# A fused attention and feed-forward kernel: normalised rows reach their columns through HBM, and the order of the projections changes

## The reference, cut to what matters

```python
query = layernorm(x) @ w_q.T + b_q          # 16 heads of 32
key_, value = ctx @ w_k.T + b_k, ctx @ w_v.T + b_v
attn = softmax(causal(query @ key_.T / sqrt(32)))
x = x + tanh(g_xattn) * ((attn @ value) @ w_o.T + b_o)
z = mx_quantize(layernorm(x))               # blocks of 32, grid of a 6 bit float
x = x + tanh(g_ffn) * (z @ mx_quantize(w_f).T + b_f)
```

## Time and profile before

| | |
|---|---|
| median of 3 runs | 1390.96 us |
| profiled execution | 1392.38 us |
| its span in the trace | 1390.6 us |
| TensorE busy | 1354.2 us, 97% |
| VectorE, GpSimd, ScalarE busy | 1124.7, 938.7, 916.6 us |
| mean granted TensorE clock | 0.989 of 2.4 GHz |

### The profile page before, as it was taken

One profiled execution on the slowest core, in us unless ns is written; L12 is line 12 of the kernel. 1 busy time (PEld: TensorE's weight loads), 2 busy tenths in 40 slices (PEclk: granted clock), 3 DMA queues, 4 the chain that ended last, 5 costly groups with the idle time before them and its releaser, 6 DMA issues.

```text
span 1390.6 us, 34895 instructions
## 1 busy us (share of the span) xinstructions
PE 1354.2 (97%) x10608; PEld 1198.5 (86%) x10608; DVE 1124.7 (81%) x4219; ACT 916.6 (66%) x2969; POOL 938.7 (68%) x1449
## 2 busy tenths in 40 slices
PE   7899999999999999999999999999999999999987
PEld 7788888898888888888888888888888889889865
DVE  5768888788888888888878878888888888888773
ACT  4667666667666666667666667666666666766661
POOL 1657776677676777676677676677677667767564
PEclk9999999999999999999999999999999999999998
DMA  8444344444444444434444434444444444443320
GB/s 253 118 112 107 103 111 124 118 129 107 109 109 120 124 128 117 107 101 119 121 126 123 108 99 115 126 119 124 110 106 109 126 118 128 110 116 99 88 62 31
DMA packets 181912, 159.10 MB, mean 114 GB/s; under 512 B 30176, under 2 KB 164320, under 8 KB 181728
## 3 DMA queue, kind: packets, MB, share of 16 engines
q1 hardware_dynamic: 181728, 156.88, 43.3%
HBM read 39.33 MB, written 16.78 MB: 40 GB/s over the span
## 4 chain that ended last, share of the span: by engine, by line
PE 59%; DVE 20%; SPq 9%; issue 5%; DMA 3%; ACT 1%; POOL 1%; DVEq 0%; ACTq 0%; POOLq 0%
PE proj L549 14%; PE proj L551 13%; PE proj L550 13%; SPq L380 9%; PE pT_ps L616 8%; DVE all_probs L891 5%; PE proj L632 3%; DMA k_stack<-k_lo 3%; DVE stats L899 3%; PE s_ps L605 3%; PE proj L660 2%; DVE all_probs L1028 2%; DVE k_lo L920 2%; PE s_ps L606 1%; DVE oT_lo L954 1%
## 5 line engine op out<-in xcount | busy, mean ns | idle before, releaser
L458 POOL TENSOR_TENSOR all_probs<-all_probs,rden 128x128 f32<-128x128 f32 (+1 forms) x1024 | 504.1, 514 | 347.5 <-DVE rden L949 346.5
L735 ACT ACTIVATE all_probs<-all_probs,neg_max 128x128 f32<-128x128 f32 (+1 forms) x1024 | 458.3, 449 | 242.4 <-DVE neg_max L891 242.2
L891 DVE CUSTOM_DVE_ANT_0 all_probs<-s_ps,causal 128x128 f32<-128x128 f32 (+1 forms) x1024 | 324.4, 354 | 144.2 <-PE s_ps L606 137.1
L616 PE MATMUL pT_ps<-ident,all_probs 128*128 128x128 f32 x1536 | 265.0, 282 | 9.9 <-POOL all_probs L458 7.2
L735 ACT ACTIVATION_READ_ACCUMULATOR all_probs<-all_probs,neg_max 128x1 f32 x1024 | 193.1, 189 | 0.0
L817 ACT ACTIVATE all_probs<-pT_ps 128x384 f32<-128x384 f32 x256 | 125.4, 490 | 87.4 <-PE pT_ps L616 87.2
L616 PEld LDWEIGHTS pT_ps<-ident,all_probs 128*128 128x128 f32 x1536 | 160.8, 142 | 25.2 <-issue 14.1
L549 PE MATMUL proj<-cT_hi,wk_hi 128*128 128x256 f32 x512 | 153.8, 300 | 1.4 <-DVE wk_lo L844 1.4
L605 PE MATMUL s_ps<-k_stack,q_stack 96*128 96x256 f32 x512 | 152.8, 299 | 2.1 <-DVE neg_max L891 2.0
L549 PE MATMUL proj<-aT_hi,wq_hi 128*128 128x256 f32 x512 | 151.0, 295 | 2.3 <-DVE aT_lo L943 2.3
L550 PE MATMUL proj<-cT_lo,wk_hi 128*128 128x256 f32 x512 | 142.7, 279 | 0.0
(11 more groups left out here) (119 smaller groups left out, 3607.9 us busy)
## 6 DMA issues: line engine op xcount, KB each, us to landing
k_stack<-k_hi SPq DMA_DIRECT2D x512, 64.0 KB, 2.0
q_stack<-q_hi SPq DMA_DIRECT2D x512, 64.0 KB, 2.1
xs_yz<-in_x SPq DMA_DIRECT2D x32, 512.0 KB, 5.2
k_stack<-k_lo SPq DMA_DIRECT2D x256, 64.0 KB, 2.0
q_stack<-q_lo SPq DMA_DIRECT2D x256, 64.0 KB, 2.1
out<-xs_yz SPq DMA_DIRECT2D x64, 256.0 KB, 2.3
c_quads<-in_ctx SPq DMA_DIRECT2D x124, 128.0 KB, 2.9
vs<-in_L_xattn_w_k SPq DMA_DIRECT2D x2, 512.0 KB, 5.8
```

The source lines that it names most:

```text
L458: last = nc.gpsimd.tensor_tensor(p, p, rden[:, sd, t, h:h + 1].to_broadcast([P, (1 + t) * P]), ALU.mult)
L616: last = nc.tensor.transpose(pT_ps[h % 2][:, m * P:(m + 1) * P], probs[:, h % P_RING, m * P:(m + 1) * P], ident[:, :])
L735: last = nc.scalar.activation(probs[:, h % P_RING, cols], probs[:, h % P_RING, cols], ACT.Exp, scale=-1.0, bias=neg_max[:, sd, t, h:h + 1] ...
L891: last = nc.vector.tensor_tensor_reduce(probs[:, h % P_RING, cols], s_ps[h % 2][:, cols], causal[:, (1 - t) * P:], 1.0, MASKED, ALU.add, A ...
```

## The change

Seven things change together.

1. xT goes from TensorE, from batch 1 on. `xn` is written to a scratch in HBM (`rows_out`, one DMA of 512 KB at the head of the step) and read back in four quadrants (`rows_back`, behind k1's pieces). VectorE turns it (`turn_rows`, slots 5 and 6), ScalarE and GpSimd make the parts (`rows_hi`, `rows_lo`, a slot and two slots later).
2. The context is loaded one step earlier (`context(i + 1)`, behind q1's pieces) and turned in slots 1 and 3.
3. k0 stands behind o1, in slots 9 and 10, q0 in slots 11 and 12, and k1 in slots 14 and 15. v1 is done a step later, in slots 1 and 2.
4. SP's order in a step is: rows out (1), x (1), k1 (12), rows back (4), q1 (12), context (4), k0 (12), results (2), q0 (12).
5. `normal_rows` goes to slot 14 of the step before, the statistics of x to slots 7 and 9, the addition of the bias to x (`XB_SLOTS`) to slots 2 and 4.
6. The weights of q are read with the columns in the order that the turned rows have.
7. 16 transposes of the identity are added at the start, while the weights arrive.

```diff
-UNITS = [("q", 1, 2), ("dT", 0, 4), ("k", 0, 1), ("dT", 1, 4), ("f", 0, 4), ("xT", 0, 1), ("f", 1, 4), ("xT", 1, 1),
-         ("o", 0, 3), ("o", 1, 3), ("q", 0, 1), ("v", 0, 1), ("k", 1, 1), ("v", 1, 1)]
-
+LAGS = {("q", 0): 1, ("q", 1): 2, ("k", 0): 1, ("k", 1): 1, ("v", 0): 1, ("v", 1): 2, ("o", 0): 3, ("o", 1): 3,
+        ("f", 0): 4, ("f", 1): 4, ("dT", 0): 4, ("dT", 1): 4}
+SLOT_WORK = ("q1 q1 q1", "dT0 q1 v1", "v1 v1 v1", "dT1", "f0 f0 f0", "f0 f1 f1", "f1 f1 o0", "o0 o0 o0", "o1 o1 o1",
+             "o1 k0 k0", "k0 k0", "q0", "q0 q0 q0", "v0 v0 v0", "v0 k1 k1", "k1 k1")
...
-SLOT_PARTS = (3, 3, 3, 1, 3, 4, 3, 3, 3, 3, 3, 1, 3, 3, 3, 2)
...
-XB_SLOTS = (5, 6)
-LN1_SLOT = SLOTS - 2
-XN_SLOTS = (1, 3)
+XB_SLOTS = (2, 4)
+LN1_SLOTS = (7, 9)
+RSTD_SLOT = 11
+XN_SLOT = 14
-TURN_SLOTS = (5, 8)
+C_SLOTS = ((1, 3), (3, 4), (4, 5))
+C_SLOTS_1 = ((12, 13), (13, 14), (14, 15))
+X_TURNS = (5, 6)
...
+            def quarters(rows):
+
+                for g in range(NQ):
+                    yield slice(g * QUAD, (g + 1) * QUAD), rows[:, g * P:(g + 1) * P].rearrange("(n l) d -> l n d", l=QUAD)
+
             def context(b):
-
-                for g in range(NQ):
-                    sp.dma_start(c_quads[g * QUAD:(g + 1) * QUAD, :, :],
-                                 ctx_in[b, :, g * P:(g + 1) * P].rearrange("(n l) d -> l n d", l=QUAD)).then_inc(
-                                     c_in, 16)
+                if b == 1:
+                    sp.wait_ge(done["cT"], T)
+                else:
+
+                    sp.wait_ge(c_turned, T * (b - 1))
+                for quadrant, rows in quarters(ctx_in[b]):
+                    sp.dma_start(c_quads[quadrant, :, :], rows).then_inc(c_in, 16)
+
+            def rows_out(b):
+                sp.wait_ge(xn_ok, T * (b + 1))
+                sp.dma_start(xn_rows.rearrange("(t p) d -> p t d", p=P), xn[:, :, :]).then_inc(xn_out, 16)
+
+            def rows_back(b):
+                sp.wait_ge(xn_out, 16 * b)
+                for quadrant, rows in quarters(xn_rows):
+                    sp.dma_start(xn_quads[quadrant, :, :], rows).then_inc(xq_in, 16)
...
             def step(i, ph):
+                if i > 1 and live(i - 1):
+                    rows_out(i - 1)
+                if at(i, 0):
+                    load_first()
+                elif live(i):
...
+                    sp.dma_start(xs[:, place(ph, 0), :, :], batch_of(x, i)).then_inc(x_in, 16)
                         sp.wait_ge(max_ok, n)
                     sp.wait_ge(left["k"], 2 * (i - 2) + 2)
                     stack("k", i - 2, 1)
...
+                if i > 1 and live(i - 1):
+                    rows_back(i - 1)
                 if live(i - 2):
 
                     sp.wait_ge(left["q"], 2 * (i - 2) + 2)
                     stack("q", i - 2, 1)
+                if i > 1 and live(i + 1):
+                    context(i + 1)
+                b = i - 1
+                if live(b):
+                    if some(b):
+
+
+                        sp.wait_ge(max_ok, HEADS * (b - 1) + HEADS // 2)
+                    sp.wait_ge(left["k"], 2 * b + 1)
+                    stack("k", b, 0)
                 if live(i - 4):
 
                     for half in range(T):
                         sp.wait_ge(left["f"], 2 * (i - 4) + half + 1)
                         sp.dma_start(out[i - 4, half * P:(half + 1) * P, :], xs[:, place(ph, 4), half, :]).then_inc(
                             out_moved, 16)
-                b = i - 1
                 if live(b):
-                    if some(b):
-
-
-                        sp.wait_ge(max_ok, HEADS * (b - 1) + HEADS // 2)
-                    else:
-
-                        sp.wait_ge(left["k"], 2 * b + 1)
-                    stack("k", b, 0)
 
                     sp.wait_ge(left["q"], 2 * b + 1)
                     stack("q", b, 0)
+                if i == 1:
+                    context(2)
 
...
+            def rows_lo(b, t):
+
+                pool.wait_ge(hi_ok["xT"], 2 * b + t + 1)
+                tok = slice(t * P, (t + 1) * P)
+                nc.gpsimd.tensor_tensor(aT_lo[:, :, tok], cols[:, t, :, :], aT_hi[:, :, tok].bitcast(F32),
+                                        ALU.subtract).then_inc(left["xT"], 1)
...
+            def rows_hi(b, t):
+
+                act.wait_ge(x_turned, T * (b - 1) + t + 1)
+                if some(n := 2 * (b - 3) + t + 1):
+
+                    act.wait_ge(done["f"], n)
+
+                act.wait_ge(done["q"], 2 * b)
+                nc.scalar.activation(aT_hi[:, :, t * P:(t + 1) * P], cols[:, t, :, :],
+                                     ACT.Copy).then_inc(hi_ok["xT"], 1)
...
+            def turn(quads, t, turned):
+
+                nc.vector.transpose(cols[:, t, :, :].rearrange("p c (n l) -> p n c l", l=QUAD),
+                                    quads[:, t * NQ:(t + 1) * NQ, :].rearrange("p n (e c) -> p n c e",
+                                                                              c=KC)).then_inc(turned, 1)
+
+            def turn_context(b, t):
                 dve.wait_ge(c_in, 16 + 16 * NQ * b)
-                if b > 1:
-
-                    dve.wait_ge(left["cT"], 2 * (b - 1) + t + 1)
-                nc.vector.transpose(cols[:, t, :, :].rearrange("p c (n l) -> p n c l", l=QUAD),
-                                    c_quads[:, t * NQ:(t + 1) * NQ, :].rearrange("p n (e c) -> p n c e",
-                                                                                c=KC)).then_inc(turned, 1)
+
+                if b > 2:
+                    dve.wait_ge(left["xT"], T * (b - 2) + t + 1)
+                elif b == 2:
+                    dve.wait_ge(left["cT"], T * (b - 1) + t + 1)
+                turn(c_quads, t, c_turned)
+
+            def turn_rows(b, t):
+                dve.wait_ge(xq_in, 16 * NQ * b)
+
+                if live(b + 1):
+                    dve.wait_ge(left["cT"], T * (b + 1) + t + 1)
+                else:
+                    dve.wait_ge(left["xT"], T * (b - 1) + t + 1)
+                turn(xn_quads, t, x_turned)
 
...
+                    if s in c_slots(i)[0]:
+                        turn_context(i, c_slots(i)[0].index(s))
+                    if s in X_TURNS and i > 1 and live(i - 1):
+                        turn_rows(i - 1, X_TURNS.index(s))
+                    if s in LN1_SLOTS and i > 0 and live(i):
+                        moments_in(i, LN1_SLOTS.index(s))
```

More of the change, by code:

```diff
@@ L99, in live, with units_of @@
         return not isinstance(b, int) or 0 <= b < B
[L101 to L104, removed]
+    def units_of(slot_work):
+        return [(s, (name[:-1], int(name[-1]))) for s, names in enumerate(slot_work) for name in names.split()]
+    assert all(sum(unit == u for _, u in units_of(SLOT_WORK)) == PARTS[unit[0]] for unit in LAGS)
     work = {}
@@ L111, in fused_kernel @@
             for s, (kind, half) in LAST_O:
-                work.setdefault((i, s), []).extend((kind, half, i - lag_of[kind, half], p) for p in range(PARTS[kind]))
+                work.setdefault((i, s), []).extend((kind, half, i - LAGS[kind, half], p) for p in range(PARTS[kind]))
         else:
[L114 to L117, removed]
+            part_of = dict.fromkeys(LAGS, 0)
+            for s, unit in units_of(SLOT_WORK_1 if i == 1 else SLOT_WORK):
+                if live(i - LAGS[unit]):
+                    work.setdefault((i, s), []).append((*unit, i - LAGS[unit], part_of[unit]))
+                part_of[unit] += 1
     work[1, 0] = [("cT", half, 0, 0) for half in range(T)] + work.get((1, 0), [])
+    work[1, 5] = [("xT", half, 0, 0) for half in range(T)] + work.get((1, 5), [])
     taken = []
@@ L541, in _ @@
             pe.wait_ge(ident_ok, 1)
-            for _ in range(WAKING):
+            for _ in range(WAKING[0]):
                 nc.tensor.transpose(proj[BANKS - 1][:, 0:P], ident[:, :], ident[:, :])
@@ L762, in unit @@
                     dst = cT_hi[:, 0] if kind == "cT" else aT_hi
-                    if kind == "cT":
-                        pass
-                    elif kind == "xT":
-                        if some(n := 2 * (b - 3) + half + 1):
-                            act.wait_ge(done["f"], n)
-                    else:
+                    if kind == "dT":
                         act.wait_ge(done["q"], 2 * (min(b + 2, B - 1) if isinstance(b, int) else b + 2) + 2)
@@ L1028, in step @@
                         nc.vector.tensor_copy(probsT[:, h % AV_HEADS, :], pT_ps[0][:, 0:3 * P]).then_inc(pT_even, 1)
-                    if s in XN_SLOTS and i > 1 and live(i - 1):
-                        normal_rows(i - 1, XN_SLOTS.index(s))
+                    if s == XN_SLOT and i > 0 and live(i):
+                        for t in range(T):
+                            normal_rows(i, t)
                     for r in range(2):
@@ L1037, in step @@
                                 stage(of, half)
-                    for t, turn_slot in enumerate(turn_slots(i)):
-                        if s == turn_slot and live(i):
```

(3 more changed lines are left out.)

93 lines of the change are left out of this document (54 added, 39 removed).

## The result

The changed kernel takes 1612.71 us (median of 4 runs, 1608.64 to 1617.06). The kernel before, on the same chip, takes 1390.55 us (4 runs, 1389.67 to 1393.0). The ratio is 1.1595, with a 95% interval of 1.1558 to 1.1632: slower by 16%. The prediction was 1566 us, with a range of 1490 to 1630; its own forecast, inside that range, was 1530 to 1600, and the result lies above it.

The account below looks back on a forecast made before the run. TensorE bound the kernel; k0's late pieces ahead of q0's in SP's queue would idle it each step. A 47.0 us step against 41.4 gave 162 us over 29 steps, 175 with start and end: 1566 us, range 1490 to 1630.

Parts of the forecast that it names:

- slot 11 to k0's first piece: In each step, VectorE hands over k0's low part and SP starts k0's pieces 2.64 us into slot 11.
- k0's pieces and the results: In SP's queue, k0's twelve issues take 8.0 us and the two results 1.5, allowing for held issues.
- q0's first six, and the landing: Behind the results, q0's sixth issue starts 3.4 us after its first; landing and TensorE's start take 2.2.
- VectorE's delay: VectorE's handover of k0 in slot 11, taken at 2.64 us; VectorE's and GpSimd's added work costed at nothing by itself.
- The clock: Behind each step's gap at slot 0, TensorE runs at the lower clock in slots 0 and 1, costing 1.6 us.
- The start: Before the 29 steps: about 6 us more in step 2; the 16 transposes cost 0, within 2 us.
- The end: After the 29 steps, the gap ahead of step 33 once more: 5.2 + 1.6, about 6.5 us.
- The base of the steps: Old step 41.4 us against a new one of 47.0; without waits the new step would be 40.09 us.
- nothing comes late: Rival: transfers land before slot 0, so TensorE never waits and the time is 1353 us; chance 0.05.
- A wait that I called gone: TensorE's 0.53 us wait for VectorE, placed in front of f0, where k0's high part waited for k1's pieces, would go.
- The queue alone at full clock: Rival: SP's queue makes the gap without lowering the clock or VectorE delay; step 45.3 us, time 1515; chance 0.17.
- The rows' way round: Rival: rows through HBM and VectorE's work delay k0 to 33 us; chain 17, step 50, time 1657; chance 0.15.

Follow-up runs that it names:

- e1: Changed kernel with the old unit order back (k0 in slots 1 and 2, q0 in 9 and 10, v1 in its own step): 1426.51 us.
- e5: Kernel before with only the unit order changed (k0 behind o1, v1 a step later), xT still on TensorE: 1554.75 us.
- e3: Changed kernel with the second half of the statistics of x in slot 12 instead of 9, its power on GpSimd in 13: 1604.15 us.
- e4: Changed kernel with 56 transposes of the identity on TensorE ahead of the scores of head 0 in each step: 1610.61 us.
- e8: e1 with the statistics of batch 1 in slots 12 and 13 of step 1 instead of 7 and 9: 1412.05 us.
- e11: e8 with the parts of k0 one slot lower, behind dT1 (three in slot 2, one in slot 3): 1357.04 us, ratio 0.975.
- e7: Changed kernel with the rows fetched from HBM between the sixth and seventh piece of k1, without added transposes: 1607.39 us.
- e9: e8 with six issues a step, context and results, moved from SP's queue to ScalarE's: 1417.41 us.

## Why the prediction was right, point by point

The sign and the range held, though the result lies above the forecast's own 1530 to 1600, and the mechanism is the one that it named: q0's pieces stand behind k0's in one queue, k0 is done two slots before q0, and TensorE waits at the scores of head 0. e1 (the order undone) and e5 (the order alone) show it from both sides. The time is 47 us above the 1566. By the prediction's own terms, measured in the profiled execution of 1617.06 us, which is 4.3 us above the median:

| term | predicted | measured |
|---|---|---|
| slot 0 to slot 11, clock included | 29.2 | 29.8 |
| slot 11 to k0's first piece | 2.64 | 3.9 |
| k0's pieces and the results | 9.5 | 9.1 |
| q0's first six, and the landing | 5.6 | 5.3 |
| the step | 47.0 | 48.06 |
| 29 steps against 41.4 | 162 | 194 |
| start | 6 | 19.3 |
| end | 6.5 | 11.2 |

- **VectorE's delay** was mis-sized most: 3.9 us for 2.64, some 35 us over 29 steps. The 2.64 us were read from a step in which VectorE followed TensorE closely. Now its maxima of slot 11 begin at 1427.67, 2.2 us after the scores. In most steps it has had no rest since the scores of slot 8, with the o units, their statistics and the statistics of x in slot 9. Those last ones are point 5 of the change, and no term of the sum had them. Without them it is 3.2 us (e3), and in e5, which keeps the old slots of VectorE's work, 2.8. The row, with the low part of k0 behind it:

```profile
1427.67 0.28 DVE L942 CUSTOM_DVE_ANT_0 all_probs<-s_ps,causal 128x128 f32<-128x128 f32 x1
...
1428.30 0.86 DVE L971 SCALAR_TENSOR_TENSOR k_lo<-proj,bias_k,k_hi 128x256 fp32r<-128x256 f32 x2
```

  The prediction had such a delay only as a rival, with a chance of 0.15: k0 ready at 33 us and a chain of 17. The date was right, since 29.8 + 3.9 gives 33.7, though by point 5 and not by GpSimd's work or the traffic, which the rival had named; the chain was 14.4.
- **The clock** was taken at 1.6 us from two gaps of 2.3 us. Behind gaps of 5 us it is 2.1 to 2.2 by slot 0 to slot 11, and 1.9 by e4. The Trainium skill (TensorE: Matmul & The Clock Gate, "HAM oscillation — how this bites in real kernels") says that a loop that waits for a DMA in each round pays for the lower clock each time. The trace agrees: 0.50 for the 4 us behind the gap that is shown, and a mean of 0.915 over the span with 31 such gaps. What the sum by terms hid, and the prediction had said, is that undoing it alone gives back only 0.3 us (e4), since the rows come no sooner.
- **The pieces** took less than allowed: 9.1 and 5.3 us for 9.5 and 5.6. Part of what VectorE cost was covered by that luck.
- **The start** was costed at nothing beside the 6 us of step 2, and that was wrong; point 5 of the change was overlooked here too. The 6 us themselves held: from slot 0 of step 2 (58.8 us instead of 45.3) to slot 11 of step 3 it is 5.8 more. The statistics of batch 1 in slots 7 and 9 of step 1 wait 11.7 us for x, VectorE prepares weights behind them, and TensorE waits for these: 13 us (e1 against e8). A later slot of step 1 removes it.
- **The end** was 11.2 us for 6.5. The gap is 4.8 and the slots behind it 2.9. Behind the last scores 3.5 more are lost at a lower clock (0.64 from 10 to 20 us behind them, 1.00 before). e8, which has no gap, has 0.63 there and loses 3.6, so the gap isn't the reason; what is stays open.
- **The base of the steps.** I set 41.4 against 47.0, and 41.36 was measured before. That the 40.09 us of a step without waits was right is shown by e11, to 0.01 us. The rival "nothing comes late", 1353 us, came near the time of a kernel that has the change with k0 in its old region: e11 is 4 us above it.
- **A wait that I called gone.** The 0.53 us of the earlier trace rows stand in front of f1, not f0 as I wrote, and are the small form of what e8 shows: k0's high part behind k1's pieces. In the change it is gone (TensorE waits for aT_lo twice in the whole span, for 2.7 us in all), because k0 stands in slots 9 and 10. So the late k0 does cure that wait. It costs twelve issues in front of q0's, which are worth far more. One slot lower in the old place (e11) nearly cures it, 2.6 us in all, for nothing.
- **The rivals.** The queue alone at full clock (1515) is excluded by the rows of the clock. The rows' way round did not decide by itself (its parts add up to 14.2 us, not the 14.4 that I wrote). e3, e4 and e7 each leave the step at 47.8, but only in e4 are the rows the reason: e7 keeps the path at the lower clock, and e3 lost nearly half of what k0's earlier handover gained to the clock. "Nothing comes late" is excluded by the 31 gaps. The section of the Trainium skill that the prediction named for it (DMA: Bandwidth & Descriptors, "Anatomy of one DMA — SWDGE (gpsimd) path") speaks of descriptors of DMAs that GpSimd issues, so it didn't bear on SP's issues. These took 0.60 us each, as in the kernel before.

## What to carry to other kernels

Where one engine issues all transfers, only one unit should have its result pass through that queue just before the next stage: two such results in a row cost the time of the first one's issues, and putting k0 seven slots ahead of q0 (e11) cost nothing here. Look also at what the moved side work delays: the statistics of x, moved by a few slots, cost 13 us at the start (e8) and made k0's pieces 0.6 us later in each step (e3). Where taking issues from a full queue changes nothing (e9), ask what its next transfer waits for. Where a buffer has one place for two halves, ask how long the second writer waits, and for what the engines behind it are waited for. A shift by one slot was worth 55 us here, and no busy share hinted at it: TensorE stood at 95% before the shift. And where two paths end within a microsecond of each other, test repairs in pairs: 2 and 5 us singly were 43 together. The last wait of the engine in which the paths meet tells which of them holds it, as in e3 and e4.

## What was not expected of the hardware

Transposes of the identity in a gap hold TensorE's clock up: 0.982 with 56 of them against 0.915 (e4). SP's issues cost the same when they are many: 0.60 us for one piece, 2.09 for four quadrants of 128 KB, in the kernel before as after. ScalarE's issues of the same transfers held it for 0.32 to 0.37 us each (e9):

```profile
690.43 0.35 ACTq L885 DMA_DIRECT2D c_quads<-in_ctx  x1
```

Open is how short the step of the changed order could become with both paths cut and no fill; that was not tried.
